# A third buffer for the B rows, narrow diagonal tap weights, and a new slot order in a fused Mamba and FP4 feed-forward layer

## What is computed

```python
x, z = split(layernorm(h) @ in_proj.T)                  # 512 + 512 channels
x = silu(conv_b + sum(xpad[:, k:k+L] * conv_w[:, k] for k in range(4)))
dt, B, C = split(x_proj[head] @ x)                      # 4 heads, 16 states
delta = softplus(dtw @ dt + dt_b);  A = -exp(A_log)
s = s * exp(delta * A) + (delta * x) * B                # one scan per state n
y = sum_n(s[n] * C[n]) + x * Dskip
h = h + (y * silu(z)) @ out_proj.T
v = fp4(layernorm(h))                                   # blocks of 16, absmax scale
out = h + fp4(silu(v @ fp4(wg).T) * (v @ fp4(wu).T)) @ fp4(wd).T
```

## Time and profile before

| what | value |
|---|---|
| median of 3 runs | 4243.98 us (4243.51 to 4249.21) |
| profiled execution | 4253.05 us, span of its instructions 4251.1 us |
| DVE busy | 4060.8 us, 96% |
| PE busy | 3945.4 us, 93% |
| POOL busy | 3941.9 us, 93% |
| ACT busy | 3639.7 us, 86% |
| DMA engines | 5 to 6 tenths busy, mean 182 GB/s |
| first scan, last scan | 84.9 us, 4152.2 us |

### The profile page before, as it was taken

One profiled execution on the slowest core, in us unless ns is written; L12 is line 12 of the kernel. 1 busy time (PEld: TensorE's weight loads), 2 busy tenths in 40 slices (PEclk: granted clock), 3 DMA queues, 4 the chain that ended last, 5 costly groups with the idle time before them and its releaser, 6 DMA issues. The chain is left out here.

```text
span 4251.1 us, 67554 instructions
## 1 busy us (share of the span) xinstructions
PE 3945.4 (93%) x19884; PEld 1859.3 (44%) x19884; DVE 4060.8 (96%) x5684; ACT 3639.7 (86%) x6807; POOL 3941.9 (93%) x2461
## 2 busy tenths in 40 slices
PE   4789999999999999999999999999999999999997
PEld 1234444444444444444444444444444444444445
DVE  6899999999999999999999999999999999999994
ACT  5888888888888888888888888888888888888874
POOL 5999999999999999999999999999999999999993
PEclk8999999999999999999999999999999999999999
DMA  3555555555555555555555555555555555555550
GB/s 107 200 192 192 186 187 191 186 189 188 185 187 190 188 185 191 184 189 191 188 184 191 184 187 190 185 185 190 192 183 190 188 186 190 189 186 187 183 184 23
DMA packets 307411, 772.79 MB, mean 182 GB/s; under 512 B 37734, under 2 KB 89062, under 8 KB 307046
## 3 DMA queue, kind: packets, MB, share of 16 engines
q1 hardware_dynamic: 305344, 766.31, 54.0%
q10 hardware_dynamic: 1702, 2.16, 0.2%
HBM read 743.16 MB, written 25.17 MB: 181 GB/s over the span
## 5 line engine op out<-in xcount | busy, mean ns | idle before, releaser
L752 POOL TENSOR_TENSOR prod<-state,cs 128x1024 f32<-128x1024 f32 x1024 | 2411.5, 2367 | 10.6 <-issue 10.3
L743 POOL TENSOR_TENSOR brow<-brow,du 128x512 f32<-128x512 f32 x640 | 817.2, 1277 | 189.6 <-DMA brow<-b_rows 179.2
L486 ACT ACTIVATE decay<-delta,aneg 128x512 f32<-128x512 f32 x1408 | 962.4, 716 | 22.5 <-DVE state L1008 20.7
L987 DVE TENSOR_TENSOR db<-db,du 128x512 f32<-128x512 f32 x1408 | 962.3, 683 | 17.8 <-PE db L1056 16.9
L1071 PE MATMUL ybank<-prod,ident 64*64 64x512 f32 x3584 | 899.3, 610 | 9.9 <-DVE hh L905 6.4
L1071 PE MATMUL cross<-prod,ident 64*64 64x512 f32 x3584 | 899.2, 610 | 0.0
L1008 DVE TENSOR_TENSOR_SCAN state<-decay,carry,db 128x512 f32<-128x512 f32 x704 | 883.1, 1263 | 0.0
L1008 DVE TENSOR_TENSOR_SCAN state<-decay,db 128x512 f32<-128x512 f32 x704 | 841.6, 1204 | 6.3 <-PE bank_b L1344 6.3
L1056 PE MATMUL db<-pieces,sel 128*128 128x512 bf16 x1408 | 541.3, 385 | 48.9 <-DVE state L1008 42.9
L486 ACT ACTIVATE db<-delta,aneg 128x512 f32<-128x512 f32 x640 | 437.8, 684 | 47.6 <-DVE state L1008 44.5
L1160 PE MATMUL bank_a<-wd,ht 128*128 128x256 f32 x1536 | 406.6, 390 | 57.7 <-ACT hh L503 56.0
(11 more groups left out here) (144 smaller groups left out, 7643.7 us busy)
## 6 DMA issues: line engine op xcount, KB each, us to landing
cs<-c_rows SPq DMA_DIRECT2D x1024, 512.0 KB, 3.7
brow<-b_rows SPq DMA_DIRECT2D x640, 256.0 KB, 3.9
xin<-in_hidden SPq DMA_DIRECT2D x128, 128.0 KB, 3.8
xres<-in_hidden SPq DMA_DIRECT2D x128, 128.0 KB, 3.8
out_x<-ot SPq DMA_DIRECT2D x128, 128.0 KB, 3.9
c_rows<-xdbl SPq DMA_DIRECT2D x128, 32.0 KB, 3.4
b_rows<-xdbl SPq DMA_DIRECT2D x128, 32.0 KB, 3.2
win<-in_win_t SPq DMA_DIRECT2D x1, 1024.0 KB, 5.1
```

The source lines that it names most:

```text
L486: act.activation(out, delta[:, w.mod(2), :], ACT.Exp, scale=aneg[:, w.mod(HEADS), n:n + 1]).then_inc(done, 1)
L743: pool.tensor_tensor(brow[:, s, :], brow[:, s, :], du[:, w.mod(2), :], ALU.mult).then_inc(db_pool, 1)
L752: pool.tensor_tensor(prod[:, r, :, :], state[:, 2 * p:2 * p + 2, :], cs[:, c, :, :], ALU.mult).then_inc(weighted, 1)
L987: dve.tensor_tensor(t[:, :], t[:, :], du[:, gu % 2, :], ALU.mult).then_inc(db_done, 1)
```

## The change

`brow` gets three buffers (`WEIGHED_ROWS = 3`). `cdiag` holds 64 columns per head and tap in place of 128: the two diagonal blocks stand above each other, made from a new tile `blocks_of_one`; `ddiag` is made in one operation per head in place of two. The last tap is two matmuls of 64 by 64 in place of one of 128 by 128. Slots and listing order on all five engines are new; the operations of a unit are otherwise the same. The core of the diff:

```diff
-WEIGHED_ROWS = 2
+WEIGHED_ROWS = 3
...
-        cdiag = sb("cdiag", [HEADS, TAPS, P])
+        blocks_of_one = sb("blocks_of_one", [Q])
+        cdiag = sb("cdiag", [HEADS, TAPS, Q])
...
# SP
-                if w := due("scan", 0):   copy_b(w, 4)
-                if w := due("scan", -6):  copy_b(w, 1)
-                if w := due("scan", -1):  spread_c(w, 0); spread_c(w, 1)
-                if w := due("scan", 3):   copy_b(w, 8); copy_b(w, 11)
+                if w := due("scan", -7):  copy_b(w, 1)
+                if w := due("scan", -4):  copy_b(w, 4)
+                if w := due("scan", -3):  spread_c(w, 0)
+                if w := due("scan", 0):   spread_c(w, 1); spread_c(w, 2)
+                if w := due("scan", 1):   copy_b(w, 8)
+                if w := due("scan", 3):   copy_b(w, 11)
...
# POOL, per unit: before
-  3: weigh 0, rstd | 4: drive 8 | 6: weigh 1 | 7: weigh 2 | 8: drive 11, v_norm, weigh 3
-  9: h_quant | 10: du | 11: weigh 4 | 13: v_quant, drive 14 | 14: weigh 5, weigh 6
-  15: drive 1', weigh 7, drive 4' | 2: h_norm
# after
+  0: weigh 7 | 1: h_norm | 3: drive 4, weigh 0, rstd | 4: weigh 1 | 5: drive 8
+  7: weigh 2, v_norm | 8: drive 11, weigh 3 | 10: du, h_quant, v_quant | 11: weigh 4
+  12: drive 14, weigh 5 | 14: drive 1' | 15: weigh 6
...
# ACT, steps 2 to 6: before
-  2: centred2, mid, decay 7 | 3: decay 9, decay 4, xnt, silu 0
-  4: pieces, var2, cross_taken, h_abs 0, v_done, silu 1, carry, delta, h_abs 1
-  6: decay 10, decay 12 | 7: decay 8, x_evac, decay 13 | 9: ..., v_abs
# after
+  2: decay 9, mid, decay 4, xnt, centred2, silu 0 | 3: carry, cross_taken, var2
+  4: h_abs 0, v_done, pieces | 5: silu 1, h_abs 1, delta
+  6: decay 10, decay 8, decay 12, x_evac | 8: v_abs, decay 13
...
# DVE
-  4: gated 0 | 5: h_up 0 | 6: h_down 0, v_max, yg, v_scales
-  7: recip, h_up 1, gated 1, h_down 1 | 9: v_up | 10: ot | 11: v_down | 12: h_max
+  4: gated 0 | 5: [h_up 0] scan, h_down 0, v_max | 6: [v_scales] scan, recip, h_up 1
+  7: [gated 1, h_down 1] scan, yg | 8: v_up | 9: v_down, ot | 13: h_max
...
# PE: after
+  0: project 1-3, sum 4, 5, spread 2, less 0 | 1: turn_h 1, spread 3, gate 0, xn_tp, sum 6
+  2: sum 7, spread 5, less 1, up 0 | 3: spread 6, gate 1 | 4: spread 7, up 1 | 5: dt
+  6: joined, down 0-3 | 7: down 4, 5, in_proj x, spread 9 | 8: spread 10
+  9: sum 0, tap 0 | 10: taps 1, 2 with sum 1, tap 3, spread 12 | 11: in_proj z, spread 13
+  12: sum 2, 3 | 13: v_tp, spread 15, x_proj, spread 0', project 0 | 15: turn_h 0
...
@@ constants on DVE
+                    for r in range(2):
+                        rows = slice(r * Q, (r + 1) * Q)
+                        dve.tensor_copy(blocks_of_one[rows, :], ident[rows, rows]).then_inc(a_ready, 1)
+                    dve.wait_ge(a_ready, 6)
...
-                            dve.tensor_scalar(cdiag[:, h, k, :], ident[:, :], cw[:, h, k:k + 1], None,
+                            dve.tensor_scalar(cdiag[:, h, k, :], blocks_of_one[:, :], cw[:, h, k:k + 1], None,
...
@@ conv_tap
-                last = pe.matmul(pbank[:, :], cdiag[:, v.mod(HEADS), k, :], x[:, k:k + CH],
-                                 start=False, stop=(k == TAPS - 1), skip_group_check=True)
+                for r in range(2):
+                    rows = slice(r * Q, (r + 1) * Q)
+                    last = pe.matmul(pbank[rows, :], cdiag[rows, v.mod(HEADS), k, :], x[rows, k:k + CH],
+                                     start=False, stop=(k == TAPS - 1), tile_position=(r * Q, r * Q),
+                                     skip_group_check=True)
```

More of the change, by code:

```diff
@@ L516, in step @@
                 u, due = timetable(b, j, n)
-                if w := due("scan", 9):
-                    decay_of(w, 15)
[L519 to L541, removed]
@@ new lines, in step @@
+                if w := due("scan", 10):
+                    decay_of(w, 15)
+                if w := due("scan", 19):
+                    keep_carry(w, 1)
+                if w := due("scan", 19):
+                    act.wait_ge(summed, w.val(PAIRS, PAIRS))
+                    wait(act, joined, w.val())
+                    act.wait_ge(conv_mm, min(w.val(plus=3), UNITS))
+                    act.activation(ycross, cross[:, :], ACT.Copy).then_inc(cross_taken, 1)
+                if t := due("post", 19):
@@ L581, in step @@
                     act.activation(v2, v2, ACT.Copy, scale=ve[:, 1, 1:2]).then_inc(v_done, 1)
[L582 to L585, removed]
                 if v := due("pre", 20):
[L587 to L597, removed]
+                    act.wait_ge(res_mm, v.val(2, 2))
+                    wait(act, b_spread, v.val(N_DVE, -N_DVE))
+                    act.activation(pieces[:, v.mod(2), :], pbank[:, :], ACT.Copy).then_inc(pieces_done, 1)
+                if w := due("scan", 6):
+                    decay_of(w, 10)
+                if w := due("scan", 6):
                     decay_of(w, 8)
-                if v := due("pre", 7):
+                if w := due("scan", 6):
+                    decay_of(w, 12)
+                if v := due("pre", 6):
                     h = v.mod(HEADS)
@@ new lines, in step @@
+                if v := due("pre", 21):
+                    h = v.mod(HEADS)
+                    act.preload_act_table_set("softplus")
+                    act.wait_ge(dt_mm, v.val(plus=1))
+                    wait(act, du_done, v.val(plus=-1))
+                    act.activation(delta[:, v.mod(2), :], pbank[:, :], ACT.Softplus,
+                                   bias=dtb[:, h:h + 1]).then_inc(delta_done, 1)
+                    act.preload_act_table_set("exp_and_others")
+                if due("post", 37) and not due("pre", 21):
+                    act.preload_act_table_set("exp_and_others")
@@ new lines, in side @@
+                if t := due("post", 70):
+                    down(t, (0, 1))
+                if t := due("post", 70):
+                    down(t, (2, 3))
+                if w := due("scan", 4):
+                    spread_b(w.val(NST, 7))
+                if t := due("post", 36):
+                    up(t, 1)
+                if v := due("pre", 18):
+                    pe.wait_ge(mid_done, v.val(plus=1))
+                    pe.matmul(pbank[:, :], less[:, 1, :], mid[:, :], start=False, stop=True,
+                              skip_group_check=True).then_inc(res_mm, 1)
@@ new lines, in side @@
+                if t := due("post", 34):
+                    up(t, 0)
+                if w := due("scan", 12):
+                    sum_up(w, (2,))
+                if w := due("scan", 12):
+                    sum_up(w, (3,))
+                if t := due("post", 29):
+                    pe.wait_ge(v_quant, t.val(plus=1))
+                    if peeled and t.val() == 0:
+                        pe.wait_ge(xnt_done, 11)
+                    else:
+                        wait(pe, h_op, t.val(2))
+                    for k in range(KM):
+                        last = pe.transpose(bank_b[:, k * P:(k + 1) * P], v2_eps[:, k * P:(k + 1) * P], ident[:, :])
+                    last.then_inc(v_tp, 1)
@@ L1310, in side @@
+                if w := due("scan", 13):
+                    spread_b(w.val(NST, 15))
                 if v := due("pre", 13):
```

554 lines of the change are left out of this document (267 added, 287 removed).

## The result

| | before | after |
|---|---|---|
| median | 4243.74 us (4236.04 to 4249.21, 4 runs) | 4127.54 us (4125.06 to 4128.27, 4 runs) |
| ratio | | 0.9726 (0.971 to 0.9743) |
| span of the profiled execution | 4251.1 us | 4123.2 us |
| DVE / PE / ACT / POOL busy | 4060.8 / 3945.4 / 3639.7 / 3941.9 us | 4036.4 / 3882.8 / 3637.1 / 3945.5 us |

The change makes the kernel 2.7% faster. The forecast was 4153 with 4130 as its low end, so the time lies 2.5 us under the range.

What follows compares the result with a forecast made beforehand. POOL's wait for a late B row held DVE 0.86 us per unit over its floor. Gains of 89 us (steady part) and 2 us (start) from 4244.0 gave 4153 us, range 4130 to 4215.

Steps and rivals of the forecast that it cites:

- low end: Best case of the range: the whole 103 us, 3 at the start, 5 at the end: 4133, less 3 for spread, 4130.
- What bounds the kernel: POOL's 1.4 us per unit wait for a late B row sets the pace; DVE stands 0.86 us over its 31.07 floor.
- Part 1: Third buffer and SP's order: row 4 issued 10.8 us before its drive, not 4.7; POOL's 1.4 us per unit wait goes.
- Part 2: New order on ACT and DVE: DVE's waits go except 0.12 us per unit; gain 0.74 x 120 = 89 us, bounds 103 and zero.
- All leads: Margins by which operations end before DVE wants their results, in the new order; the shortest were put at 0.4 us.
- 0.12 us taken as left: DVE wait assumed to remain per unit, about a third of the shortest lead, cutting the gain from 0.86 to 0.74.
- Rival 1: A new wait: one close coupling missed by 0.4 us per unit in the mean; 46 us gained, 4198 us; chance 0.17.
- Rival 3: DVE's v_max, moved ahead of scan 6, waits for v_done: slower by 29 us, 4273 us; chance 0.12.
- Part 3: Last tap in quarters on PE: they run beside each other, 0.86 to 0.9 us, work unchanged, between 0 and +0.05 us.
- lead (d): PE's last tap and spread 12 end before DVE's product for state 12: 5.5 against 6.3 us, lead 0.7, early 0.5.
- Part 4: Start and end: DVE's diagonal weights take 3.4 us, not 5.39, so 2 us less (0.5 to 3); end unchanged, 5 either way.
- The end: About 99 us of latency chains after the last scan, order within a unit unchanged: 0, with 5 us either way.

Runs made afterwards that it cites:

- E10: Kernel before with one SP statement moved, the copy of row 4 to step 15 ahead of two C copies: 4147.82 us, 0.9686 of before.
- E4: Changed kernel with two B row buffers in place of three: 4126.02 us, 0.9711 of before.
- E9: Kernel before with only SP's new order; two buffers, wide weights, full last tap: 4134.60 us, 0.9656 of before.
- E6: Changed kernel with one more table load on ACT, ahead of decay 12: 4260.38 us, 0.9949 of before.
- E7: Changed kernel with h_abs 1 put back behind delta on ACT: 4176.82 us, 0.9766 of before.
- E3: Changed kernel with SP's queue alone in the old order: 4323.71 us, 1.0176 of before.
- E5: Changed kernel's orders on all engines with the old parts (two buffers, 128-column weights, full last tap): 4127.60 us, 0.9652 of before.
- E1: Kernel before with three B row buffers, narrow weights and quartered last tap, no slot moved: 4241.28 us, 0.9989 of before.

## Why the prediction was right and wrong

**What bounds the kernel: right.** DVE's floor of 30.61 and 31.53 us was reached to the hundredth. The cause in the queue is shown by E10, which moved that one copy.

**Part 1: right in its mechanism, wrong in what it credited.** The copy of row 4 is issued 10.3 us ahead of its drive, 10.8 were worked out, and the wait is gone. But I argued from "with three buffers", and E4 and E9 show that two are enough. With two, in E4, the copy does wait for a scan and is issued 5.6 us ahead of its drive in place of 10.3 (medians), but it lands after 3.2 us, still in time. The closest row is row 1: in E4 it is issued 3.7 us ahead of its drive and lands after 3.4, where after has 8.5 us and 4.2. So the third buffer buys room and no time.

**Part 2: the positions were right, the deduction from them was not.** For a late unit, counted from scan 0:

| step | forecast | in the trace of after |
|---|---|---|
| v_done ends, v_max starts | 8.4, 10.6 | 8.5, 10.6 |
| h_abs 1 ends | 11.1 | 11.2 |
| decay 8 ends | 15.7 | 15.8 |
| v_abs ends, v_up starts | 17.2, 17.8 | 17.3, 17.8 |
| spread 12 ends, its product starts, behind the start of yg | 5.5, 6.3 | 5.6, 6.3 |

v_up on DVE and the last tap on PE show two of these places:

```profile
2063.46 0.39 DVE L911 SCALAR_TENSOR_TENSOR hw<-bank_b,v_eps 128x256 f32<-128x256 bf16 x1
```

```profile
2251.32 1.03 PE L1083 MATMUL pbank<-xearly,cdiag 64*64 64x512 f32 x4
2252.28 0.39 PE L1058 MATMUL db<-pieces,sel 128*128 128x512 bf16 x1
```

The first is in unit 64, an early one, 17.29 us behind its scan 0. All leads held and no rival happened. The term "0.12 us taken as left", 14 us over 120 units, was put in as a caution, with no row that showed such a rest; it measured zero. Rival 1 (4198 us) named a mechanism that works as it says: E6 and E7 show the price that it would have had. Rival 3 looked for a slower kernel at v_max, 29 us over before. A slower one could be made from this change (E3, 75 us over), but in another place, SP's order against POOL's.

**Part 3: right.** From the first quarter of the last tap to spread 12 it is 2252.28 - 2251.32 = 0.96 us, where the full tap took 0.86 and 0.86 to 0.9 were forecast; lead (d) stayed at 0.7, and no stall comes of it. The 0.10 us more belong to the new place and not to the quarters, for the full tap takes the same 0.96 us there, in E5:

```profile
2255.24 1.13 PE L1078 MATMUL pbank<-xearly,cdiag 128*128 128x512 f32 x2
2256.20 0.38 PE L1055 MATMUL db<-pieces,sel 128*128 128x512 bf16 x1
```

E5 also has the same time as after. In the old place the quarters are slower, 1.01 us in E1 against 0.86 in before (medians). By the rule of the Trainium skill ("TensorE: Matmul & The Clock Gate", "Part 3: Packing small matmuls — row/col tiling") an estimated 0.3 us per unit of bare weight load would have come on top. The trace disagrees in the new place, where the quarters cost nothing more than the full tap; in the old place they cost 0.15 us, half of that.

**Part 4: right for DVE's stretch, not shown for the start, too narrow at the end.** From the first diagonal weight to what follows the last, DVE takes 43.42 - 39.73 = 3.69 us:

```profile
39.73 0.40 DVE L1028 COPY blocks_of_one<-ident 64x64 f32<-64x64 f32 x2
...
43.42 2.28 DVE L866 TENSOR_TENSOR state<-state 88x2048 f32<-88x2048 f32 x1
```

This is 1.7 us less than the 5.39 of the earlier trace rows; 2 were forecast. But that it lies on the path to the first scan was assumed and doesn't show: the start is no shorter with narrow weights over all profiles. That it was 3.1 us shorter in this pair is luck. The end was put at 0, with 5 either way, because of chains "whose order within a unit stays the same". The change did give these chains a new order; from the last scan on it became 7.9 us shorter, of which about 5 come with the new order of the other engines.

**The sum.** The span was forecast at 4160 and came to 4123.2, 37 less:

| term | forecast | measured | missed |
|---|---|---|---|
| steady part, excess over the floor | 0.86 x 120 = 103 | 0.91 x 120 = 109 | 5.6 |
| left over in it | 0.12 x 120 = 14 | 0 | 14.4 |
| units 0 to 7 | not in the sum | 8.1 | 8.1 |
| start | 2 | 3.1 | 1.1 |
| from the last scan on | 0 | 7.9 | 7.9 |

The excess over the floor was 0.91 and not 0.86 because I took the unit of before, 31.93 us, from 2000 us of the trace; its mean over units 8 to 126 is 31.98.

The largest miss of the forecast itself is the 14 us taken as left. The step that put the time outside the range is the low end's: "takes the whole 103 us, 3 at the start and 5 at the end". It was to be the case in which all goes well, and it left out units 0 to 7, in which the same queue feeds the same drives. Their 8 us alone would have brought 4130 to 4122. I had counted only the units in which all four jobs run, because only for these I knew the floor; as an estimate, the bound for the others should have been the same 0.86 us each, 7 us. The rest of what the low end missed in the span is 5.8 us of the steady part and 2.9 at the end. Against these misses stands one that went the other way, by luck: the span of the profiled execution of before was 7 us over its median, that of after 4 us under its own, so the medians moved by 116 us where the spans moved by 128.

## What to carry to other kernels

Where an engine waits for a transfer, look first at what stands ahead of that transfer in its issuing queue and what that waits for; one more buffer doesn't help a copy that is issued late, and here moving one copy in the queue brought the steady part to within 1.4 us of what the whole change, on five engines, made of it (109 us less). Once one engine never waits, a unit takes its work to the hundredth, so put the low end of a range at that floor in every stretch where the engine runs, the first and last units too, and take off only what a row shows. And try each of two matched listings alone: here the new one on SP lost nothing in the steady part without its partners, and the new ones on the other engines without it made the kernel 1.8% slower than it was before.

## What the runs showed of the hardware

- A B row of 256 KB landed 3.1 to 4.05 us after its issue in before for states 1, 8, 11 and 14, but 4.64 us for state 4 (medians). The page's median over all rows, 3.9 us, hid that. Standing some 0.4 us behind a C copy of 512 KB doesn't explain it: row 4 does so in after too and lands after 4.1 us, and row 1 in before after 4.04. Over all kernels the medians go from 3.15 to 4.98 us; why is open.
- The kernel before, which waits for such a landing, took 4244 to 4282 us on three chips, and 4276 and 4282 us at two times on one of them. Five kernels that hardly wait for it lie within 9 us of each other, each on one chip only.
- What a table load costs ACT is more than its record: 1.28 us in the record, 1.38 from start to start, since the operations beside it no longer overlap (E6). An engine that waits starts 0.03 us behind the end of the record that it waits for.
- DVE ran 119 units in a row without an idle gap beside POOL at 98% and DMA engines at 6 tenths, and no operation of a unit became longer by more than 3 ns in the mean: the scan without a carried state has 1193 ns in after and 1204 in before.
- The length of a DVE record isn't what the operation costs. In E5's profile this scan's records are 1390 ns long and the product's 872 (672 in after), and still its units take 30.60 and 31.51 us, as in after.
